# An AdaLN/FFN kernel with MXFP4 rounding: residual of two tiles a group by identity products, last group tile by tile

## What is computed

```
w = table[cond]                                  # (64, 64, 64)
y = einsum('bct,bcd->bdt', x, w)                 # mix the 64 channels of each sample
a = quant_dequant_mxfp4(y); wq = quant_dequant_mxfp4(weight)   # weight is 512 x 512
out = x + a @ wq.T + bias                        # 4096 rows of 512
```

## Time and profile before

| | us |
|---|---|
| median of 3 runs (99.6 to 100.2) | 99.98 |
| the profiled execution's own time | 99.33 |
| its span, first to last instruction | 97.7 |
| PE busy (share of span) | 81.4 (83%) |
| DVE busy | 83.0 (85%) |
| ACT busy | 77.9 (80%) |
| POOL busy | 33.0 (34%) |
| mean granted PE clock | 0.98 of full speed |
| DMA: 23.74 MB, of it q0 (issued by POOL) | 6.31 MB, 30.8% of the 16 engines' span |
| the adding DMA of 768 KB, issue to landing, median | 8.2 |

### The profile page before, as it was taken

One profiled execution on the slowest core, in us unless ns is written; L12 is line 12 of the kernel. 1 busy time (PEld: TensorE's weight loads), 2 busy tenths in 40 slices (PEclk: granted clock), 3 DMA queues, 4 the chain that ended last, 5 costly groups with the idle time before them and its releaser, 6 DMA issues.

```text
span 97.7 us, 2302 instructions
## 1 busy us (share of the span) xinstructions
PE 81.4 (83%) x736; PEld 43.2 (44%) x744; DVE 83.0 (85%) x136; ACT 77.9 (80%) x82; POOL 33.0 (34%) x62
## 2 busy tenths in 40 slices
PE   5999696998929998998899899979999997699300
PEld 4965362792913353336334533623393343344000
DVE  1269999999999999599999999999999899985500
ACT  4750788799999889999999999999989959874000
POOL 4274669988557547303000200300030030054000
PEclk9999999999999999999999999999999999999965
DMA  2987979894879898999999994599059939989994
GB/s 29 352 318 228 284 203 301 191 346 124 281 231 281 214 306 174 326 283 215 259 250 371 394 221 91 219 324 206 9 220 331 201 113 304 242 204 223 345 329 180
DMA packets 13852, 23.74 MB, mean 243 GB/s; under 512 B 4114, under 2 KB 4626, under 8 KB 13842
## 3 DMA queue, kind: packets, MB, share of 16 engines
q1 hardware_dynamic: 11216, 17.31, 53.7%
q0 software_dynamic: 2624, 6.31, 30.8%
q10 hardware_dynamic: 2, 0.00, 0.0%
HBM read 10.49 MB, written 8.39 MB: 193 GB/s over the span
## 4 chain that ended last, share of the span: by engine, by line
PE 31%; issue 21%; ACT 16%; POOL 8%; DVE 8%; DMA 6%; POOLq 4%; ACTq 0%; DVEq 0%
PE o_ps L306 13%; PE y_ps L271 7%; DMA mix<-in_L_cond_weights_dram 6%; POOL bias L238 5%; ACT zone L422 4%; ACT y_sb L413 4%; ACT aT L439 3%; PE o_ps L296 3%; POOLq L172 3%; ACT o_sb L430 3%; PE y_ps L306 3%; PE o_ps L323 3%; PE o_ps L300 2%; ACT z L405 2%; POOL mix L175 2%
## 5 line engine op out<-in xcount | busy, mean ns | idle before, releaser
L306 PE MATMUL o_ps<-wT,aT 128*128 128x512 bf16 x98 | 23.5, 380 | 1.0 <-issue 1.0
L323 PE MATMUL o_ps<-idle 128*128 128x128 bf16 x296 | 22.2, 231 | 1.2 <-DVE idle L579 1.2
L323 PEld LDWEIGHTS o_ps<-idle 128*128 128x128 bf16 x296 | 18.3, 103 | 9.1 <-issue 4.7
L271 PE MATMUL y_ps<-x_sb,mix 64*64 64x512 f32 x128 | 16.8, 610 | 5.9 <-ACT y_sb L413 2.9
L175 POOL DMA_DIRECT2D mix<-in_L_cond_weights_dram x32 | 17.4, 544 | 12.2 <-issue 10.9
L422 ACT ACTIVATE zone<-inv 128x2048 int16<-128x2048 int16 (+1 forms) x10 | 17.5, 1764 | 4.2 <-DVE inv L541 4.2
L548 DVE TENSOR_TENSOR n_int<-y_sb,inv 128x1024 int16<-128x1024 f32 x16 | 19.4, 1218 | 0.2
L439 ACT COPY aT<-o_ps 128x1024 bf16<-128x1024 bf16 x16 | 15.7, 1038 | 2.8 <-PE o_ps L296 2.8
L245 POOL DMA_DIRECT2D x_sb<-o_sb x6 | 5.3, 883 | 35.8 <-ACT o_sb L430 35.8
L405 ACT ACTIVATE z<-y_ps 128x1024 bf16<-128x1024 bf16 x16 | 16.3, 1041 | 1.4 <-PE y_ps L271 1.4
L413 ACT COPY y_sb<-y_ps 128x1024 f32<-128x1024 f32 x16 | 16.3, 1034 | 0.0
(11 more groups left out here) (38 smaller groups left out, 56.3 us busy)
## 6 DMA issues: line engine op xcount, KB each, us to landing
x_sb<-in_x_dram SPq DMA_DIRECT2D x7, 1024.0 KB, 6.1
x_sb<-o_sb POOLq DMA_DIRECT2D x6, 768.0 KB, 8.2
out_dram<-x_sb SPq DMA_DIRECT2D x6, 768.0 KB, 4.1
out_dram<-x_sb SPq DMA_DIRECT2D x10, 256.0 KB, 5.4
w_sb<-in_L_ffn_weight_dram SPq DMA_DIRECT2D x4, 256.0 KB, 3.0
x_sb<-in_x_dram SPq DMA_DIRECT2D x2, 512.0 KB, 6.5
out_dram<-x_sb POOLq DMA_DIRECT2D x4, 256.0 KB, 3.7
mix<-in_L_cond_weights_dram POOLq DMA_DIRECT2D x32, 16.0 KB, 4.3
```

Of the source, the lines that this page charges most:

```text
L271: last = nc.tensor.matmul(y_ps[HALVES[g], 2 * q + r, :], mix[HALVES[r], (step - 1) * GROUP + n, :], x_tiles(step, n)[HALVES[r], :], start= ...
L306: last = nc.tensor.matmul(o_bank(step, t), aT[:, t, c, :], wT[:, c, :], start=False, stop=(c == KC - 1))
L323: nc.tensor.matmul(o_ps[:, 2, c * P:(c + 1) * P], idle[:, :], idle[:, :], start=True, stop=True)
```

## The change

Six edits. Tile 3, not tile 0, is now added by DVE (`ADDED = 3`), and only tile 2 by DMA (`SUMMED = 2`, 256 KB). Tiles 0 and 1 of groups 1 to 6 get x by `residual_pair` before their products; ACT copies the pair straight over x (`copy_pair`), and SP stores it in two DMAs through the exchanged view. These products stand where `keep_busy(14)` stood (for group 1 after the `keep_busy(20)` of step 1), and the transposes of that pair are no longer put back in place ("straight"). The transposes use banks 2 and 3. The bias is split by POOL, the table loads of step 4 go ahead of its DMAs, and there are 6 of these instead of 12. The last group is mixed in two quadrants, not four, unexchanged, and then rounded, transposed, copied and multiplied tile by tile. In the weight's rounding the third and fourth tile are taken singly. The diff, cut to its core:

```diff
--- before.py
+++ after.py
...
-ADDED = 1
+
+SUMMED, ADDED = 2, 3
...
-            return ADDED * (min(step, LAST - 1) - 1)
+            return min(step, LAST - 1) - 1
...
-            return o_ps[:, 2 * q + 1, :].bitcast(BF16)
+            return o_ps[:, 2 + q, :].bitcast(BF16)
...
-            return o_ps[:, 2 * t, :] if t < 2 else y_ps[:, t - 2, :]
+            return o_ps[:, t, :] if t < 2 else y_ps[:, t - 2, :]
...
-                sp.wait_ge(added, adds_before(step) + ADDED)
-                store(step, 0, ADDED)
+                sp.wait_ge(pair_copied, 2 * step)
+                for g in range(2):
+                    sp.dma_start(exchanged_dram[step - 1, 0, g, :, :, :].rearrange("r c t -> c r t"),
+                                 x_tiles(step, 0, 2)[HALVES[g], :].rearrange("p (r t) -> p r t", r=2)
+                                 ).then_inc(stored, 16)
+                sp.wait_ge(added, adds_before(step) + 1)
+                store(step, ADDED)
                 sp.wait_ge(x_added[step % 2], 16 * ((step + 1) // 2))
-                store(step, ADDED, GROUP - ADDED)
+                store(step, SUMMED)
             for t in range(GROUP):
                 sp.wait_ge(added, adds_before(LAST) + t + 1)
                 store(LAST, t)
-            sp.wait_ge(stored, 16 * (2 * (LAST - 2) + GROUP))
+            sp.wait_ge(stored, 16 * (4 * (LAST - 2) + GROUP))
...
+
+            pool.wait_ge(bias_in, 16)
+            nc.gpsimd.tensor_copy(bias_b[:, 0, :], bias_f[:, 0, :]).then_inc(bias_step, 1)
+            pool.wait_ge(bias_step, 1)
...
+            nc.gpsimd.tensor_copy(bias_b[:, 1, :], bias_f[:, 1, :]).then_inc(bias_step, 1)
+            pool.wait_ge(bias_step, 3)
+            nc.gpsimd.tensor_tensor(bias_b[:, 2, :], bias_f[:, 1, :], bias_b[:, 1, :], ALU.subtract
+                                    ).then_inc(bias_step, 1)
+            load_mixes(pool, mybir.EngineType.Pool, pool_mix_in, 4, POOL_TILES)
             pool.wait_ge(bias_step, 4)
-            for t in range(GROUP):
+            for r in range(2):
                 for i in range(3):
-                    pool.dma_start(bias3[32 * t + i:32 * t + i + 1, :], bias_b[:, i, :]).then_inc(bias3_in, 16)
-            for step in range(4, STEPS + 1):
+                    pool.dma_start(bias3[32 * r + i:32 * r + i + 1, :], bias_b[:, i, :]).then_inc(bias3_in, 16)
+            for step in range(5, STEPS + 1):
                 load_mixes(pool, mybir.EngineType.Pool, pool_mix_in, step, POOL_TILES)
 
             for step in range(1, LAST - 1):
 
-                pool.wait_ge(copied_out, (GROUP - ADDED) * step)
-                pool.dma_start(x_tiles(step, ADDED, GROUP - ADDED), o_sb[:, step % 2, :, :].rearrange("p t n -> p (t n)"),
-                               accum_op=ALU.add).then_inc(x_added[step % 2], 16)
+                pool.wait_ge(copied_out, step)
+                pool.dma_start(x_tiles(step, SUMMED), o_sb[:, step % 2, :], accum_op=ALU.add
+                               ).then_inc(x_added[step % 2], 16)
...
@@ -266,6 +284,14 @@
                 if step > 1:
 
                     pe.wait_ge(y_copied, tiles_done(step - 1, 2 * q + 1))
+                if step == LAST:
+
+                    for n in (2 * q, 2 * q + 1):
+                        for half in HALVES:
+                            last = nc.tensor.matmul(y_ps[half, n, :], mix[half, (step - 1) * GROUP + n, :],
+                                                    x_tiles(step, n)[half, :], start=True, stop=True)
+                        last.then_inc(y_ready, 1)
+                    return
...
             def residual_pair(step, q):
 
+                if 1 < step < LAST - 1:
+
+                    pe.wait_ge(pair_copied, 2 * (step - 1))
                 for r, g in QUARTERS:
                     nc.tensor.matmul(o_bank(step, 2 * q + r)[HALVES[g], :], ident_f[HALVES[r], :],
                                      x_tiles(step, 2 * q + g)[HALVES[r], :], start=True, stop=False)
...
-                    pe.wait_ge(copied_out, (GROUP - ADDED) * (step - 2) + 2 * q + 2 - ADDED)
+                    if q == 0:
+                        pe.wait_ge(copied_out, step - 1)
+                    else:
+                        pe.wait_ge(added, adds_before(step))
...
+            def turn_last(t):
+                pe.wait_ge(a2_done, LAST + t + 1)
+                if t >= 2:
+
+                    pe.wait_ge(aT_ready, tiles_done(LAST, t - 2))
+                for c in range(KC):
+                    last = nc.tensor.transpose(t_pair(t % 2)[:, c * P:(c + 1) * P], a2[:, t, c * P:(c + 1) * P],
+                                               ident[:, :])
+                last.then_inc(t_ready, 1)
...
             def bias_tile(step, t, start=True):
-                nc.tensor.matmul(o_bank(step, t), ones[32 * t:32 * t + 3, :], bias3[32 * t:32 * t + 3, :],
-                                 start=start, stop=False)
+                row = t % 2 * 32
+                nc.tensor.matmul(o_bank(step, t), ones[row:row + 3, :], bias3[row:row + 3, :], start=start, stop=False)
 
             def ffn_tile(step, t):
-                pe.wait_ge(aT_ready, tiles_done(step, t // 2 * 2 + 1))
+                pe.wait_ge(aT_ready, tiles_done(step, t if step == LAST else t // 2 * 2 + 1))
                 for c in range(KC):
                     last = nc.tensor.matmul(o_bank(step, t), aT[:, t, c, :], wT[:, c, :], start=False,
...
             def ffn_pair(step, q):
                 pe.wait_ge(aT_ready, tiles_done(step, 2 * q + 1))
-                if q == 0 and step > 1:
-
-                    pe.wait_ge(added, adds_before(step))
                 for t in (2 * q, 2 * q + 1):
-                    bias_tile(step, t)
+
+                    bias_tile(step, t, start=(q == 1))
...
             mix_pair(3, 0)
             for step in range(1, LAST):
                 if step == 2:
-                    pe.wait_ge(ident_f_ready, 2)
                     pe.wait_ge(ones_ready, 1)
-                    pe.wait_ge(bias3_in, 16 * GROUP * 3)
+                    pe.wait_ge(bias3_in, 16 * 2 * 3)
                 if step > 1:
                     for q in range(2):
                         ffn_pair(step - 1, q)
@@ -352,18 +391,17 @@
 
                         pe.wait_ge(y_copied, tiles_done(LAST, 2 * q + 1))
                         residual_pair(LAST - 1, q)
-                if step > 1:
-
-                    pe.wait_ge(copied_out, (GROUP - ADDED) * (step - 2) + 3 - ADDED)
-                if step < LAST - 1:
+                if step == 1:
                     keep_busy(14)
+                elif step < LAST - 1:
+                    residual_pair(step, 0)
                 pe.wait_ge(a2_done, step + 1)
                 for q in range(2):
-                    turn_pair(step, q, straight=(step == LAST - 1))
+                    turn_pair(step, q, straight=(q == 0 or step == LAST - 1))
                 if step == 1:
                     keep_busy(20)
-                if step == LAST - 2:
-                    keep_busy(12)
+                    pe.wait_ge(ident_f_ready, 2)
+                    residual_pair(step, 0)
                 if step + 3 <= LAST:
                     mix_pair(step + 3, 0)
...
-            pe.wait_ge(a2_done, LAST + 1)
-            turn_pair(LAST, 0)
+            turn_last(0)
             ffn_tile(LAST - 1, 3)
 
-            pe.wait_ge(added, adds_before(LAST - 1))
-            pe.wait_ge(copied_out, (GROUP - ADDED) * (LAST - 2))
+            pe.wait_ge(pair_copied, 2 * (LAST - 2))
             bias_tile(LAST, 0)
             bias_tile(LAST, 1)
+            turn_last(1)
             ffn_tile(LAST, 0)
-            pe.wait_ge(a2_done, LAST + 2)
-            turn_pair(LAST, 1)
+            turn_last(2)
             ffn_tile(LAST, 1)
 
             pe.wait_ge(late_copied, 2)
             bias_tile(LAST, 2)
             bias_tile(LAST, 3)
+            turn_last(3)
             ffn_tile(LAST, 2)
             ffn_tile(LAST, 3)
...
-            def copy_out(step, t, n):
-                if t == ADDED and step > 2:
+            def copy_pair(step):
+                act.wait_ge(o_ready, tiles_done(step, 1))
+                nc.scalar.copy(x_tiles(step, 0, 2).rearrange("p (t n) -> p t n", t=2), o_ps[:, 0:2, :]
+                               ).then_inc(pair_copied, 2)
+
+            def copy_out(step):
+                if step > 2:
 
                     act.wait_ge(x_added[step % 2], 16 * ((step - 1) // 2))
-                act.wait_ge(o_ready, tiles_done(step, t + n - 1))
-                nc.scalar.copy(o_sb[:, step % 2, t - ADDED:t - ADDED + n, :], o_ps[:, t:t + n, :]).then_inc(copied_out, n)
+                act.wait_ge(o_ready, tiles_done(step, SUMMED))
+                nc.scalar.copy(o_sb[:, step % 2, :], o_ps[:, SUMMED, :]).then_inc(copied_out, 1)
...
                                ).then_inc(aT_ready, 2)
+
+            def copy_turned_last(t):
+                act.wait_ge(t_ready, GROUP * LAST + t + 1)
```

(81 more changed lines are left out.)

5 lines of the change are left out of this document (4 added, 1 removed).

## The result

The change makes the kernel about 1% faster: 99.05 us median against 100.01, 20 runs each, ratio 0.989 (0.987 to 0.992). The forecast was 98.5 against 99.98, a gain of 1.5; the gain is 0.96.

The account below looks back on a forecast made before the run. No engine bounds the whole; ACT and DVE are both full in the like steps, so gains come only where both had waited. Terms -1.17 + 1.95 - 0.87 - 1.4 = -1.5 take 99.98 to 98.5 us, range 96.5 to 100.2.

Parts of the forecast that it names:

- Step 2, load order: Step 2: table loads ahead of bias DMAs let PE mix group 4 earlier; gain 1.17 us with the head in it.
- POOL's bias operations: Before step 2's loads: four bias operations on POOL take 0.38 us each, 1.5 in all, bounds 0.2 and 1.5 each.
- the slack: Step 2: POOL's DMAs land before PE needs them, with 1.7 us to spare for the bias, 2.7 for the loads.
- Rival B: Head of step 2: POOL's bias operations wait out DVE operations, PE waits for bias rows; 101.6 us, chance 0.10.
- Head: Weight rounding: the third tile's maximum fills DVE's idle time and bias operations leave DVE; gain 0.35 us.
- Steps 5 and 6: Group 8's mixing in two quadrants makes each pair 0.9 us longer, identity products add 0.2; loss 1.95 us passed on.
- Rival A: Group 8's mixing: two quadrants cost little, only the identity products' 0.2 us remains; 96.7 us, chance 0.15.
- Weight loads: Group 8's mixing: by the skill's rule each pass adds a load, some 0.2 us a pair; the forecast went without.
- Last group: From the last group's first rounding: tile by tile, PE finishes and the last add runs earlier; gain 0.87 us.
- End: Behind the last add: fewer stores of group 6 left, so 4.3 us instead of 5.7; gain 1.4, bounds 0.3 and 2.2.
- the 4 us that the prediction named as its sign: End of the kernel: the last store landing within 4 us of the last add would show the forecast right.
- Rival C: End: gives nothing, as late stores of group 7 and the four last ones fill the DMAs; 99.9 us, chance 0.14.

Follow-up runs that it names:

- quads: The changed kernel with group 8 mixed in four quadrants instead of two, its halves left exchanged in the output; 97.58 us against 99.42.
- four_and_pairs: The changed kernel with group 8 mixed in four quadrants, halves put back, and its last group done two tiles at a time; 97.72 us, ratio 0.969.
- tail_pairs: The changed kernel with its last group rounded, transposed and copied two tiles at a time, as in the kernel before; 99.02 us, ratio 0.983.
- late_left_out: The changed kernel without POOL's four late stores, so group 7 is missing from the output; 96.44 us against 99.42.
- load_order: The kernel before with only POOL's table loads of step 4 put ahead of its 12 bias DMAs; 99.88 us against 100.20.

## Why the prediction was right, step by step

**Step 2, load order: right.** Forecast 1.17 with 0.35 of it from the head, so 0.82 from here; measured 0.80 at `limit` 3 and 1.04 at `limit` 6, as for the order alone. That 1.04 is the whole wait that DVE had before `limit` 3. PE mixed group 4 at 28.87, 5.77 after `limit` 1 and not 6.79 as before.

**POOL's bias operations: taken at 1.5 us, measured 2.25** (15.17 to 17.42), inside the slack. Changed kernel, POOL, and DVE's `rescale` of the weight:

```profile
15.17 0.82 POOL L243 CAST bias_b<-bias_f 16x32 bf16<-16x32 f32 x1
...
16.08 0.56 POOL L245 TENSOR_TENSOR bias_f<-bias_f,bias_b 16x32 f32<-16x32 f32 x1
...
16.70 0.36 POOL L248 CAST bias_b<-bias_f 16x32 bf16<-16x32 f32 x1
...
17.14 0.28 POOL L250 TENSOR_TENSOR bias_b<-bias_f,bias_b 16x32 bf16<-16x32 f32 x1
...
19.02 2.27 POOL L176 DMA_DIRECT2D mix<-in_L_cond_weights_dram  x4 [1.59 <-issue]
```

```profile
14.70 1.23 DVE L620 TENSOR_TENSOR a<-n_int,top 128x2048 bf16<-128x2048 int16 x1
```

The first cast, 16 x 32 values, lasts 0.82 and ends 0.06 after DVE's operation. In `quads` that DVE operation ends at 15.47, and the same cast, begun at 15.18, lasts 0.35:

```profile
14.24 1.23 DVE L615 TENSOR_TENSOR a<-n_int,top 128x2048 bf16<-128x2048 int16 x1
```

```profile
15.18 0.35 POOL L243 CAST bias_b<-bias_f 16x32 bf16<-16x32 f32 x1
```

When DVE stands still they are short. In `four_and_pairs` it waits 0.74 us from 15.95 on, and the second and the third operation are:

```profile
16.10 0.23 POOL L245 TENSOR_TENSOR bias_f<-bias_f,bias_b 16x32 f32<-16x32 f32 x1
...
16.39 0.20 POOL L248 CAST bias_b<-bias_f 16x32 bf16<-16x32 f32 x1
```

The rule that I let speak against the change (Trainium skill, "SBUF — State Buffer", section "SBUF: two separate sides": a port pair shared and held exclusively) is borne out, in my reading: a held operation ends just behind DVE's. It cost only 0.75 us over my figure, since only the rest of a DVE operation was waited for each time, and nothing of it reached PE, which went from the mixing to the bias rows of step 2 without a wait. Rival B had the mechanism and not the price.

**Head: wrong by 0.4.** Forecast a gain of 0.35. From the end of ACT's last z of the weight to `invert` it was 2.89 before and 3.00 now, and the bias gives 0.07: no gain. The third tile's tree was to fill a wait, but the z of tiles 3 and 4 came back to back in this profile. In `tail_pairs` and `late_left_out`, where the fourth came alone and late, the same stretch is 2.26 and 2.20. So the edit can gain 0.6, and whether it does hangs on when the weights land.

**Steps 5 and 6: mechanism right, size 0.3 too large.** Forecast +1.95, measured +1.63 from `limit` 6 to `limit` 7 (+1.39 from `limit` 3, with the 0.24 of DVE's pace in it), of which two quadrants are 1.57 (10.76 against 9.19 in `quads`). Each pair took 1.93 (forecast 1.9), ACT waited 1.50 before the second `z_pair` (71.97, shown under `quads`; forecast "some 1.5"). Rival A is out: `quads` shows the price.

Two things made it smaller. The identity products ran beside the mixing, so both together took 2.73 us (69.93 to 72.66) and not 2.9. And the second pair began only 0.7 us later than in `quads`, measured from `limit` 3, and not 0.9. In the steps before, DVE and not ACT set the pace (no wait at its `limit` of groups 3 to 6).

**Weight loads.** By the rule on row groups (Trainium skill, "TensorE: Matmul & The Clock Gate", section "The mechanism") each pass would have carried its load. The eight records of a two-quadrant pair span 1.93, that is 1.73 for four passes plus the last one's latency of about 0.2 (one record lasts 0.65, and the next in the same quadrant starts 0.43 behind it): no room for it. The loads themselves, two at a time, lie beside the pass that runs in the same quadrants, so here the trace does not agree with the rule:

```profile
64.21 0.17 PEld L291 LDWEIGHTS y_ps<-x_sb,mix 64*64 64x64 f32 x2 [0.26 <-issue]
...
64.64 0.17 PEld L291 LDWEIGHTS y_ps<-x_sb,mix 64*64 64x64 f32 x2 [0.26 <-issue]
```

**Last group: -0.87 forecast, -0.77 measured,** right in itself. What I missed is its coupling to the end: it was given back there (`tail_pairs`).

**End: the step that failed in size.** Forecast 1.4 ("3.6 for the last ... 4.3 instead of 5.7"), measured 0.7: the last store took 4.3 us to land and not 3.6, outside the 4 us that the prediction named as its sign. I counted SP's stores out of the way, rightly (the last one is issued at 92.53, right behind the add at 92.50; before, 1.4 us behind). With the last group in pairs the term would have held: the end is 3.8 in `four_and_pairs` against 5.6 in `load_order`, a gain of 1.8. What the forecast left out is that its own step before, the last group tile by tile, brings POOL's last two late stores 0.9 us nearer to the last add, and that stretches the end by 1.0 to 1.2 (5.0 against 4.0 in `tail_pairs`, and against 3.8 in `four_and_pairs`). The late stores are as large as the others, 256 KB, and cost the end of the changed kernel 2.6 in all. Rival C, an end that gives nothing, came true by half.

Sum of the measured stages: -1.04 + 1.63 - 0.77 - 0.7 = -0.88, and with +0.11 - 0.07 of the head -0.84. The medians differ by 0.96 in the first measurement and 0.78 in the second, so the terms close to about 0.1. That the total missed by no more than 0.5 owes something to luck: the 0.3 too much for steps 5 and 6 hides nearly half of the 0.7 that the end fell short.

## What to carry to other kernels

Where two engines are full in the steady part, moving work there was worth nothing (53.39 us against 53.31); look at where both wait once, and at the end. Finishing the arithmetic sooner pays only if the stores behind it do not share the DMAs with stores that the same edit delays: check how far ahead of the last one they leave. And 64 x 64 products were cheap only while all four quadrants were used: a pair with unexchanged output, in two, took 1.93 us instead of 1.04. The best kernels here that write the whole output in its right places keep the new residual and drop both of the change's edits to group 8 (97.72 and 96.89 us).

## What was not expected of the hardware

The last store of 256 KB took 2.0 us to land without POOL's four late stores and 4.3 with them. Stores whose output begins with a dimension of 2 moved 51 GB/s at a DMA share of 0.13, and SP was held 6.8 us by a pair of such issues instead of 1.26. A cast of 16 x 32 values on POOL lasted from 0.20 to 0.82 us, by what DVE was doing.
